# Shares of the projection's products over the steps of the attention rounds: two of five patterns of one table

## The reference

```python
mod = jax.nn.silu(condition) @ Wada + bada
sh_a, sc_a, gt_a, sh_m, sc_m, gt_m = jnp.split(mod, 6, axis=1)
xm = _layernorm(x, g1, be1) * (1.0 + sc_a[:, None, :]) + sh_a[:, None, :]
x = x + gt_a[:, None, :] * _attention(xm, Wqkv, Wproj, bproj)      # causal softmax
xm = _layernorm(x, g2, be2) * (1.0 + sc_m[:, None, :]) + sh_m[:, None, :]
h = jax.nn.gelu(xm @ W1 + b1, approximate=False)
x = x + gt_m[:, None, :] * (h @ W2 + b2)
```

## Time and profile before

| | |
|---|---|
| time, median of 3 runs | 3148.65 us (3148.61 to 3149.07) |
| the profiled execution, its own time | 3149.18 us |
| its span, first to last instruction | 3147.5 us |
| mean granted TensorE clock | 0.999 |
| busy: PE, PEld (weight loads), DVE, ACT, POOL | 98%, 77%, 78%, 45%, 54% |

### The profile page before, as it was taken

How to read it: one execution, slowest core, us unless ns; L and a number is a source line. 1 busy time by engine, 2 the same in 40 slices (tenths; PEclk the granted TensorE clock), 3 DMA queues, 4 the chain that set the end, 5 groups by cost and what they waited for, 6 DMA issues and landing times.

```text
span 3147.5 us, 64741 instructions
## 1 busy us (share of the span) xinstructions
PE 3099.2 (98%) x22888; PEld 2417.4 (77%) x22888; DVE 2451.6 (78%) x2975; ACT 1429.7 (45%) x2876; POOL 1704.9 (54%) x1385
## 2 busy tenths in 40 slices
PE   8999999999999999999899999999999999999999
PEld 5677777777777777766688888888888888888888
DVE  5688887787888778766787878878787787878874
ACT  4355555555555555566543333333333333333333
POOL 3388888888888888888742323232322322323232
PEclk9999999999999999999999999999999999999999
DMA  7666566666656666676713222221222313222120
GB/s 251 211 191 193 170 193 183 177 188 184 194 174 187 183 177 187 181 192 178 180 41 81 57 63 68 52 80 46 74 57 63 79 41 80 57 63 67 53 67 14
DMA packets 304625, 391.81 MB, mean 124 GB/s; under 512 B 24296, under 2 KB 206088, under 8 KB 304448
## 3 DMA queue, kind: packets, MB, share of 16 engines
q1 hardware_dynamic: 292336, 371.86, 41.7%
q10 hardware_dynamic: 12112, 17.42, 1.6%
HBM read 270.66 MB, written 118.00 MB: 123 GB/s over the span
## 4 chain that ended last, share of the span: by engine, by line
PE 90%; DVE 5%; issue 2%; DMA 1%; ACT 1%; POOL 1%; SPq 0%; DVEq 0%; ACTq 0%; POOLq 0%
PE psY L1025 22%; PE psH L1013 14%; PE psA L793 9%; PE psT L847 9%; PE psH L1016 7%; PE psA L885 7%; PE psA L797 6%; PE psP L922 6%; PE psS L816 4%; DVE mx L1379 2%; PE psA L858 2%; PE psA L765 1%; DVE psS L1375 1%; PE psA L907 1%; PE psA L902 1%
## 5 line engine op out<-in xcount | busy, mean ns | idle before, releaser
L1654 POOL TENSOR_TENSOR h_l<-h_full,h_h 128x256 fp32r<-128x256 f32 x512 | 451.2, 881 | 1099.5 <-ACT h_h L1255 1099.5
L1117 ACT ACTIVATE e<-psT 128x512 f32<-128x512 f32 (+1 forms) x1202 | 605.6, 555 | 377.0 <-PE psT L847 373.6
L1379 DVE TENSOR_REDUCE mx<-psS 128x4 f32<-128x2048 f32 (+3 forms) x384 | 665.9, 1755 | 118.6 <-PE psS L816 80.5
L1252 ACT ACTIVATE h_full<-h_full,b1c 128x256 f32<-128x256 f32 x512 | 260.4, 509 | 995.1 <-DVE h_full L1555 995.1
L1013 PE MATMUL psH<-a_l,w1p_h 128*128 128x512 f32 x2048 | 547.7, 389 | 1.0 <-ACT o_sb L1125 0.8
L1555 DVE TENSOR_REDUCE h_full<-psH 128x256 f32<-128x512 f32 x512 | 346.8, 677 | 238.8 <-PE psH L1016 230.6
L1712 POOL TENSOR_TENSOR es<-e 128x512 f32<-128x512 f32 (+1 forms) x242 | 444.9, 1839 | 159.5 <-ACT e L1117 75.6
L1013 PEld LDWEIGHTS psH<-a_l,w1p_h 128*128 128x128 f32 x2048 | 384.1, 188 | 83.1 <-ACT o_sb L1125 1.0
L847 PEld LDWEIGHTS psT<-qst,kst 97*128 97x128 f32 x2404 | 349.1, 189 | 113.7 <-issue 70.2
L847 PE MATMUL psT<-qst,kst 97*128 97x256 f32 (+1 forms) x2404 | 410.4, 290 | 3.4 <-ACT e L1117 1.7
L1025 PE MATMUL psY<-w_h,h_h 128*128 128x512 f32 x1024 | 404.2, 395 | 0.8 <-POOL h_l L1654 0.8
(11 more groups left out here) (118 smaller groups left out, 4927.5 us busy)
## 6 DMA issues: line engine op xcount, KB each, us to landing
qk_split<-qk_hl SPq DMA_DIRECT2D x128, 512.0 KB, 3.6
kst<-qk_split SPq DMA_DIRECT2D x128, 256.0 KB, 3.9
qst<-qk_split SPq DMA_DIRECT2D x128, 256.0 KB, 4.1
xin<-in_x_dram SPq DMA_DIRECT2D x64, 256.0 KB, 3.6
values<-vout ACTq DMA_DIRECT2D x64, 256.0 KB, 2.4
kmx<-qk_split SPq DMA_DIRECT2D x32, 512.0 KB, 4.7
qmx<-qk_split SPq DMA_DIRECT2D x32, 512.0 KB, 5.8
kst<-qk_split SPq DMA_DIRECT2D x128, 128.0 KB, 3.9
```

The source lines that it names most:

```text
L1117: act.activation(e[:, s % ERING, 2 * hp:2 * hp + 2, 0:w], score_bank(s, hp, with_a)[:, :, 0:w], ACT.Exp, scale=SCALE).then_inc(sem("exp_do ...
L1252: act.activation(h_full[:, m % 4, :], h_full[:, m % 4, :], ACT.Gelu, bias=b1c[:, m:m + 1])\
L1379: reduce = dve.tensor_reduce(mx[:, part, :, qt], psS[:, :, col:col + w], AX_X, ALU.max)
L1654: return pool.tensor_tensor(dst, full, high.bitcast(F32), ALU.subtract)
```

## The change

```diff
-A_SHARES = ((6, 0, 6), (2, 8, 2), (6, 0, 6), (1, 5, 1, 5), (2, 8, 2), (5, 1, 5, 1)) * 2
+A_SHARES = ((6, 0, 6), (4, 8, 0), (6, 0, 6), (1, 5, 1, 5), (4, 8, 0), (6, 0, 6, 0)) * 2
```

## The result

The changed kernel takes 3185.64 us (median of 4 runs, 3183.58 to 3190.7), the kernel before 3148.63 beside it: a ratio of 1.0119, 95% interval 1.0106 to 1.0133. That is 37 us more; forecast were 33 us more, 3182 us. Of the four executions of one later kernel (items 1 and 7 back) one took 3380.83 us at a granted clock of 0.849 and is left out of its ratio.

A forecast was written before the change was run, and what follows sets the result against it. PE's own stream was taken to bound rounds 0 to 11. Per round +1.25 - 0.2 + 1.2 + 0.8 - 0.24 - 0.2 = +2.6 us; twelve (31.3) plus 1.8 gave +33.1 on 3149.18: 3182 us, range 3156 to 3194.

The forecast's parts named there:

- Step 9: PE waits 1.25 us for maxima, as `a_high` of item 1 in step 5 is stopped by POOL's add.
- Step 11: PE's existing wait before this step's maxima goes: -0.2 us a round.
- Step 23: PE waits 1.2 us (0.6 to 1.9), with item 5's `a_high` in step 19 ahead of both `normalise`.
- Step 29: PE waits 1.0 us, taken as 0.8, as item 7's `a_high` in step 25 is stopped by POOL's add.
- The shorter steps: Four product moves a round on PE, steps 17, 19, 37, 39, save time: -0.24 us.
- The earlier copies: Bank free a step earlier, so PE's bank wait shrinks by 0 to 0.35 us a round, taken as -0.2.
- The rounds: Sum of the terms: +2.6 us for each of rounds 0 to 11, 1.8 for round 12.
- Only steps 9 and 29: Rival: no wait at step 23, as the third and fourth `normalise` slip through: +18.6, 3168 us; chance 0.14.
- one wait a round: Rival: PE late from step 9, so step 25's add is over before DVE comes: +8, 3157 us; chance 0.08.
- Faster, if `a_high` came ahead of the add: Rival: `a_high` precedes POOL's add in step 5, no wait, only gains: -8 us, 3141; chance 0.09.
- Gains and short waits cancel: Rival: DVE restarts quicker than its rows say, 3149 us; chance 0.08.
- SP: Item 1's store moves ahead in the queue and delays step 8's loads by a step or so: no cost.

The follow-up runs named there:

- items 1 and 7 back: Changed kernel with `a_high`, `a_low` and store of items 1 and 7 returned to their earlier steps 7, 8, 9 of their group: 3178.15 us, ratio 1.0092.
- item 5 back: Changed kernel with `a_high`, `a_low` and store of items 5 and 11 returned to the places of the kernel before: 3177.52 us, ratio 1.009.
- items 4 and 5 back: Changed kernel with `a_high`, `a_low` and stores of items 4, 5, 10, 11 returned to the places of the kernel before: 3175.26 us, ratio 1.0086.
- the reduction form: `a_high` as a `tensor_reduce` over a length-one axis: 3142.71 us in the kernel before, 3142.12 in the changed, 3140.11 with new shares and old places.

## Why the prediction was right

**Step 9.** 1.25 us forecast, 1.27 measured, and by the mechanism named: the reduction done at 21.27 us from the round's start, against 21.29 (996.22 - 974.93) in the prediction. The 0.55 us between the add's end and `a_high`'s came again at every place. By the rule of the Trainium skill (SBUF — State Buffer, "Who interferes with whom"), with a full 0.68 behind the add, it would have been 1.38; the measured 1.27 decides for the row.

**Step 11.** -0.2 forecast, -0.22 measured.

**Step 23.** 1.2 forecast, 1.5 measured, in the range given there (0.6 to 1.9). The choice between its ends was wrong: the case "DVE comes late from step 17, since `veps` is behind `a_high` of item 4" is the one that came, with half of its price; the runs with item 5 back, and with items 4 and 5 back, show that it is item 4. I had mentioned it and not put it in the sum, and the order that the sum stood on, `a_high` of item 5 ahead of the add, did not come.

**Step 29.** 0.8 forecast; 0.69 in nine of rounds 1 to 11, and none in the two in which PE was slow in step 23. The run with items 4 and 5 back shows 1.27 there, so the reason given (PE is held up before and POOL is not) holds; it is step 23 that holds it up, not step 9. The size is in part luck: with PE in time the wait was forecast as 1.0 and is 1.27, and the hold-up takes 0.58 off it where 0.2 was allowed. Of these 0.27, 0.23 are POOL's add, which comes 3.81 us behind the start of step 25 in round 9 of that run, where the kernel before (4.05) less the 0.47 of the shorter step gives 3.58.

**The shorter steps.** -0.24 forecast; -0.06 in each of 16/17, 36/37 and 38/39 and the same is contained in 18/19: right in size. All of the shares' effect, measured with the reduction form, is -0.32, of which 0.05 is a wait at step 19 that stays in 3 of 12 rounds with the shares of before.

**The earlier copies.** -0.2 for a bank wait that would go: wrong. The row of that wait, one place a round, is 3.9 us in 11 rounds before and after. Another 0.3 came that I had not seen, at step 19, whose last sums no longer wait for POOL.

**The rounds.** Together +2.62 us for a round like 3 to 11 (94.75 against 92.13), where +2.6 was forecast. That it fits so closely is luck: 0.3 too little at step 23 and 0.2 for the bank wait that stayed stand against 0.3 at step 19 and 0.1 at step 29. Rounds 0 to 2 are 0.9 longer than that. Round 0 was 0.7 longer in the kernel before as well (92.86); what makes it so in rounds 1 and 2, PE's lower clock behind the wait of step 23, was no term of the sum. Round 12 is +2.9 instead of +1.8: its steps 9 and 29 wait 1.40 and 1.45 us, as PE comes there in time, and the shares bring nothing in it. 33.4 + 2.9 = 36.3, where the sum had 33.1. (The forecast's own range of 3168 to 3194 does not quite follow from its bounds: 12 x 1.8 + 1.8 and 12 x 3.7 + 1.8 give 3172 and 3195.) The spread of the timed runs, 7 us against 1 before, fits rounds with and without the clock's fall (the four runs' clocks are 0.994 to 0.999, the lowest in the longest run), but only the profiled one shows its rounds, so this is argued and not shown.

**The rivals.** "Only steps 9 and 29" and "one wait a round" are refuted by the rows; nearest to the first is the run with items 4 and 5 back. "Faster, if `a_high` came ahead of the add" failed on the order that it named: `a_high` starts 0.28 us behind the add. "Gains and short waits cancel" asked for a quicker restart than the 0.55 that came everywhere. *SP:* no cost forecast and none seen, for PE's waits of rounds 1 to 11 have no line for a load.

## What to carry to other kernels

Before an instruction is moved, look at what runs on the neighbour engine at the moment in which it will start, not only at its own length: 0.68 us of work took 2.64 here because it came 0.28 us after an add. In a chain without slack, as the maxima are here, every such delay becomes a wait of the engine that bounds the kernel, and the delays of several items act on each other along the chain (a late PE also shortens the next wait), so all of it must be worked out from the first. And where rows show such a meeting, ask first for a form of the same operation that does not meet the other engine: with it the kernel before gains 6 us, and the places that cost 37 cost nothing.

## What the runs showed of the hardware that I had not expected

A wait of PE between busy stretches can cost more than its length. The waits of more than 0.9 us for maxima in rounds 0 to 12 of all profiled runs, with PE busy before and behind, measured from the starts of scores and maxima: behind 103 of up to 1.44 us PE kept its speed every time. Of 3 of 1.47 us, one was followed by a slow stretch; of 12 of 1.51 to 1.56 at step 23 (11 in the changed kernel, one with items 1 and 7 back), two; of 11 of some 1.62 with items 1 and 7 back, 7; of 13 of 2.3, 10. Each time PE lost 0.8 to 1.6 us. Waits of one length and at one place were followed by it in some rounds and not in others, so the length alone does not decide; what else does is left open.
